# In the last recurrence, the sum of input and state for the output goes from VectorE to GpSimd

## The reference, cut to what matters

```
x = x + L0(x);  x = x + L1_scan(x);  x = x + L2_experts(x)
def step(h, z_t):                                   # layer L3, z = x, h starts as cond_1024
    gate = sigmoid(h @ Wh.T + z_t @ Wz.T + b)
    h_new = tanh(h * (1 - alpha) + gate * z_t)
    return h_new, h_new
x = x + scan(step, cond_1024, x)                    # out = input + state, at each of 2048 times
```

## Time and profile before

| | |
|---|---|
| median of three runs | 2017.97 us (2017.9 to 2018.12) |
| the profiled execution's own time | 2022.03 us |
| its span | 2020.2 us |
| leaky recurrence, from its first bulk to the end | 1713.75 to 2020.2 us |
| busy over the span | PE 97%, DVE 55%, ACT 40%, POOL 7% |
| granted TensorE clock in the leaky recurrence | 1.00 (2.4 GHz) |

### The profile page before, as it was taken

How to read it: one execution, slowest core, us unless ns; L and a number is a source line. 1 busy time by engine, 2 the same in 40 slices (tenths; PEclk the granted TensorE clock), 3 DMA queues, 4 the chain that set the end, 5 groups by cost and what they waited for, 6 DMA issues and landing times. The chain is left out here.

```text
span 2020.2 us, 45685 instructions
## 1 busy us (share of the span) xinstructions
PE 1963.6 (97%) x18180; PEld 1185.1 (59%) x18180; DVE 1104.9 (55%) x2342; ACT 800.6 (40%) x1685; POOL 142.5 (7%) x144
## 2 busy tenths in 40 slices
PE   7999979999999999999999999999999999999997
PEld 4999954444444444444444444444455555999996
DVE  4566646544797545111111147554755664778887
ACT  3444445423121333343333345322332332566564
POOL 0000000000000100111111111111111110000000
PEclk8999989999999999999999999999999999999999
DMA  7033337765242423999998965533332352101111
GB/s 294 13 117 133 125 110 202 217 193 146 105 167 104 146 104 112 231 202 207 202 203 204 197 199 177 157 89 89 94 87 81 100 154 93 44 3 43 42 42 44
DMA packets 281903, 266.38 MB, mean 132 GB/s; under 512 B 225991, under 2 KB 233293, under 8 KB 275086
## 3 DMA queue, kind: packets, MB, share of 16 engines
q1 hardware_dynamic: 270942, 228.73, 39.5%
q0 software_dynamic: 10800, 35.40, 6.5%
HBM read 153.70 MB, written 56.36 MB: 104 GB/s over the span
## 5 line engine op out<-in xcount | busy, mean ns | idle before, releaser
L1036 PE MATMUL sh_p<-xh,arena 128*128 128x512 f16 x2048 | 611.2, 380 | 8.9 <-DVE xl L1290 7.4
L1036 PE MATMUL sh_p<-xl,arena 128*128 128x512 f16 x1024 | 389.2, 380 | 0.0
L1036 PEld LDWEIGHTS sh_p<-xh,arena 128*128 128x128 f16 x2048 | 200.7, 98 | 252.3 <-issue 11.5
L1051 PE MATMUL p<-sh_h_hi,arena 128*128 128x512 f16 x1024 | 304.6, 379 | 0.0
L1791 DVE SCALAR_TENSOR_TENSOR ro_hs<-ro_h,fac,ro_hs 128x512 f16<-128x512 f32 x71 | 53.3, 751 | 307.2 <-ACT ro_hs L1777 293.5
L1205 ACT CAST sh_h_hi<-sh_half_h 128x512 f16<-128x512 f32 x128 | 79.1, 618 | 348.1 <-DVE sh_half_h L1556 341.3
L1734 PE MATMUL ro_pf<-arena,xres 128*128 x852 | 200.7, 387 | 7.4 <-PEq L870 4.0
L1199 ACT ACTIVATE sh_sig<-sh_p,fac 128x512 f32<-128x512 f32 x128 | 87.8, 686 | 291.5 <-PE sh_p L1036 291.5
L1734 PE MATMUL ro_py<-arena,ro_ht 128*128 x852 | 195.7, 380 | 0.7 <-DMA ro_ht<-ro_hs 0.7
L1051 PE MATMUL p<-sh_h_lo,arena 128*128 128x512 f16 x512 | 194.1, 379 | 0.0
L1553 DVE SCALAR_TENSOR_TENSOR sh_half_h<-sh_sig,sh_p 128x512 f32<-128x512 f32 x128 | 87.7, 685 | 153.9 <-ACT sh_sig L1199 153.6
(11 more groups left out here) (273 smaller groups left out, 3124.9 us busy)
## 6 DMA issues: line engine op xcount, KB each, us to landing
stage<-in_shared_w SPq DMA_DIRECT2D x29, 768.0 KB, 5.4
routed_rows<-xres SPq DMA_DIRECT2D x71, 256.0 KB
stage<-in_norms_r SPq DMA_DIRECT2D x16, 1024.0 KB, 4.9
stage<-in_routed_w SPq DMA_DIRECT2D x16, 1024.0 KB, 4.9
stage<-in_norms SPq DMA_DIRECT2D x14, 1024.0 KB, 5.4
arena<-x SPq DMA_DIRECT2D x12, 1024.0 KB, 6.1
rnn_xs<-in_x SPq DMA_DIRECT2D x8, 1024.0 KB, 18.7
x<-xres SPq DMA_DIRECT2D x16, 512.0 KB, 2.6
```

The lines of the kernel that those rows point to most:

```text
L1036: mm = nc.tensor.matmul(p1[u % P1][:], arena[:, w:w + P], x[slot(gl)][:, :, k, :], start=(j == 0), stop=(j == 3 * KD - 1))
L1051: mm = nc.tensor.matmul(p2[m][:], arena[:, w:w + P], h[n % 2][:], start=(i == 0 and j == 0), stop=(i == HID - 1 and j == 2))
```

## The change

GpSimd gets a `chunk` function of its own, that runs through the full rounds of the leaky recurrence: for each of the four steps it waits until both halves of `hist` of that step are written, and adds input and state into `xo`. The fourth add of a chunk raises `summed`. Ahead of the first it waits, as VectorE did, until the store of the buffer two chunks back has landed. VectorE leaves the add and that wait out in this layer (`not leaky`); the first recurrence is as it was. The lines below the new function move down by 13.

```diff
@@ block.gpsimd
+                def chunk(q, p, c, o, u, ahead):
+                    if o is None:
+                        return
+                    wait_alone(pool, stored[p], (u + 1) * 16, 16)
+                    for j in range(CHUNK_STEPS):
+                        cols = slice(j * LANES, (j + 1) * LANES)
+                        wait_alone(pool, h32_ready, (q * CHUNK_STEPS + j + 2) * parts, parts)
+                        add = nc.gpsimd.tensor_tensor(xo[p][:, :, cols], xs_chunk(c)[:, :, cols], hist[p][:, :, cols], ALU.add)
+                    add.then_inc(summed, 1)
+
+                if leaky:
+                    over_rounds(pool, lambda: warm_chunks(chunk), lambda r: full_chunks(pool, r, chunk))
@@ block.vector
-                        if o is not None:
+                        if o is not None and not leaky:
                             if j == 0:
                                 wait_alone(dve, stored[p], (u + 1) * 16, 16)
                             add = nc.vector.tensor_tensor(xo[p][:, :, cols], xs_chunk(c)[:, :, cols], hist[p][:, :, cols], ALU.add)
```

## The result

| | before | changed kernel |
|---|---|---|
| median | 2018.76 us (18 runs, 2015.34 to 2022.42) | 2023.61 us (18 runs, 2020.46 to 2025.05) |
| ratio to before, 95% interval | | 1.0023 [1.0016, 1.0030] |
| span of the profiled execution | 2020.2 us | 2020.7 us |
| first to last hd of the leaky recurrence | 1723.88 to 2012.91: 289.03 us | 1719.94 to 2012.97: 293.03 us |

The change makes the kernel slower, by 0.23% or some 4.6 us. The spans of the two profiled executions differ by only 0.5 us, because the layers ahead of the leaky recurrence, which nothing touches, took 3.94 us less in the second one (the first hd at 1719.94 against 1723.88). So in what follows each kernel is read twice: by its ratio over many runs, and by the distance from its first to its last hd, 91 steps, which the layers ahead cannot move. By that measure the change costs 4.00 us.

The account below looks back on a forecast made before the run. It took TensorE as the bound, with waits for x_lo at chunk boundaries. Per chunk 0.28 + 3 x 0.13 = 0.67 us, 9.4 over 14 chunks: 2022.03 + 9.4 = 2031.4, less 4.06 gives 2027.4; range 2019 to 2039.

Parts of the forecast that it names:

- the hold of about one add: VectorE stands still while GpSimd's add reads SBUF, held 0.61 us where its own add took 0.33; chance 0.38.
- Removed, 7.0 or 5.6 us: Dropping VectorE's 64 adds ends TensorE's wait for x_lo at 14 chunk boundaries: -7.0 us, or -5.6 by TensorE's own wait.
- no disturbance: Rival: VectorE and GpSimd run freely side by side, a chunk goes towards 12.43 us, time 2011.5 us; chance 0.33.
- How long the add takes: One GpSimd add of 256 elements, estimated from fills: 0.53 us, with 0.31 and 0.74 as ends.
- H = 0.61: Time VectorE is held per GpSimd add: 0.53 us for the add plus 0.08 of lost overlap with the preceding instruction.
- The boundary, +0.28 a chunk: At each chunk boundary x_lo comes 0.61 - 0.33 = 0.28 us later, all of it on the path.
- The three other steps, +0.13 each: In a chunk's three non-boundary steps gz comes 0.28 us later, less 0.15 of slack on VectorE: 0.13 each.
- The room of 0.15 us: VectorE's slack between the earliest possible start of x_lo's successor, 1908.58, and gz's start at 1908.73.
- Chunks 14 and 15 and the tail at 0: Last two chunks cost nothing, covered by extra room; the ending check costs 0, within 0.4 us either way.
- Shared reading: Rival: both engines advance, VectorE loses 0.43 us for two input streams where it won 0.33; 2019.4 us, chance 0.15.
- The slow GpSimd: Rival: the add is itself held up and lands in gz and arg, or holds VectorE 0.8 us and more; 2039 to 2044, chance 0.14.
- the chunk of 13.6 us: Sign: distance between first bulks of two chunks in the changed kernel, 13.6 us; 12.4 to 12.6 if nothing disturbs.

Follow-up runs that it names:

- e1_no_add: Changed kernel with GpSimd's adds left out, its waits kept and one element written a chunk: ratio to before 0.9980, 284.63 us from first to last hd.
- e8_late: Changed kernel with GpSimd's whole add also waiting for x_lo of its step: ratio to before 1.0098, 305.98 us from first to last hd.
- e6_halves: Changed kernel with GpSimd's add split into two halves, behind hist's first half and behind x_lo: ratio to before 1.0013, 291.06 us first to last hd.
- e3_copy: Changed kernel with GpSimd copying hist into the output buffer instead of adding: ratio to before 0.9988, 287.38 us from first to last hd.
- e4_other: Changed kernel with GpSimd adding two tensors that nobody else touches: ratio to before 1.0020, 293.19 us from first to last hd.

## Why the prediction was right, and where its sizes were off

The forecast was slower, by GpSimd's add holding VectorE, 2027 us with 2019 to 2039 as its own range. Measured: 2023.61, on a before of 2018.76. The forecast of +9.4 us became +4.6 by the ratio and +4.00 by first to last hd. The direction and the mechanism held: VectorE stands still beside GpSimd's add, and loses more than it won. The size was about twice too large. The prediction gave a slower kernel 0.49 and the hold of about one add 0.38, and its range began at 2019, next to no change.

- *Removed, 7.0 or 5.6 us.* Too much. Without any add the layer is 4.4 us shorter (e1_no_add). The comparison of a warm-up with a full chunk, on which the 7.0 rested, contained 0.17 us a chunk that belongs to the loop. The waits of TensorE, 5.6 us, were nearer. This sized the rival of no disturbance and not the forecast, but it means that the best case was 2017.97 - 4.4 = 2013.6 and not 2011.5.
- *How long the add takes.* 0.53 us was too short. With no VectorE instruction running at its start the add takes 0.73 to 0.74 (e8_late), which is the prediction's upper end, three streams at the rate of the fills. Behind hd it takes 1.01.
- *H = 0.61.* Measured: 0.53 to 0.54. That this is close is luck, since two errors nearly cancel. The add is 0.2 us longer than I took it. Against that, only what is left of it counts when the held instruction begins (0.67 to 0.68 us), and 0.14 us of the held instruction pass beside it, where I had put 0.08 on top. With the add's true length the same working gives H = 0.82, and 2039. VectorE loses 0.54 where it won 0.33, that is 0.21 and not 0.28.
- *The boundary, +0.28 a chunk.* x_lo is 0.21 us later and the bulk with it (1.34 us after hd, for 1.14 before): +0.20. The step rises from 3.53 to 3.70 and its neighbour from 3.21 to 3.23.
- *The three other steps, +0.13 each.* This is where most of the size was lost. The room of 0.15 us was right: gz is 0.06 later, of which TensorE's spare 0.02 takes its part, and the step goes from 3.09 to 3.13. But only two steps of a chunk have it; the one at the boundary's other side, 3.21 to 3.23 before, is 3.23 and is counted above. So 0.07 for two steps and not 3 x 0.13. A chunk costs 0.20 + 0.07 = 0.27, fourteen 3.8 of the 4.00.
- *Chunks 14 and 15 and the tail at 0.* Confirmed: but for the boundary step in chunk 14, one of the fourteen, their steps are 2.98 to 3.07 us as before. The last hd is held, and the check ends at 2015.82, 2.85 us after the last hd began, for 2.45 before: 0.4 us, at the bound that I gave. It comes on top of the 4.00 and makes 4.4, close to the 4.6 of the ratio.
- *The rivals.* No disturbance is excluded by every row above. Shared reading, 0.43 for two streams, is excluded by the ends: the second engine's instruction always comes to its end a fixed time after the first one's. The slow GpSimd did not come, although the adds do last 1.01 us in the loop: they stand still behind hd first, and what is left of them when x_lo begins is 0.68.

Of the signs that I named, the chunk of 13.6 us came out at 13.20, the waits for x_lo at 0.6 or 0.7 us each for 0.7 to 0.8, and the adds at 0.73 to 1.01 for 0.5 to 0.7. The idle gap ahead of a held instruction did not appear: the loss lies within the durations.

## What to carry to other kernels

In these runs work that was moved from VectorE to GpSimd was free only where GpSimd didn't read SBUF while VectorE ran an instruction with two SBUF inputs. The price was what was left of GpSimd's instruction when VectorE's began, less 0.14 us. It is paid by the VectorE instruction that comes behind, so look at which one that is and whether the chain waits for it. To find out what a hold depends on, compare the ends of the two instructions: their durations change with every tenth of a microsecond at the start. Before moving work to another engine, look whether its place in the queue is what costs: here the same add on the same engine behind its neighbour cost nothing. And compare like with like: a stretch in a loop and one written out can differ by more than the term in question.

## What was not expected of the hardware

- VectorE's hold is shorter than GpSimd's instruction by the lead that GpSimd has and by 0.14 us more: 0.53 us beside an add of 0.76 (two inputs of 128x256 f32), 0.20 beside a copy of 0.46, nothing beside a fill of 0.31.
- Which of the two engines waits changes with 0.1 us: in the changed kernel, with the two starts within 0.01 us of each other, the add ran 1.01 us and x_lo 0.96; with the add ahead by 0.09 it ran 0.76 and hd 0.95.
- From x_lo on VectorE to GpSimd's next instruction it took 0.23 to 0.26 us in the loop (1904.26 to 1904.49 in e6_halves) and mostly 0.17 outside it, from hist on ScalarE 0.24 and 0.14. To TensorE's bulk it was 0.05 us from VectorE's x_lo in the changed kernel (1896.96 to 1897.01). The extra 0.1 us in the loop is missing in e3_copy and e4_other, which don't read xs; that working out its address is the cause wasn't tried by itself.
